# Weights of the edges loaded behind the first three node loads, and prepared one part per node pair

## The reference

```python
q = (x @ Wq + bq).reshape(n, H, C)            # H = 8 heads of C = 32
k = (x @ Wk + bk).reshape(n, H, C)
v = (x @ Wv + bv).reshape(n, H, C)
e = (edge_attr @ We).reshape(-1, H, C)
kj = k[src] + e
alpha = jnp.einsum('ehc,ehc->eh', q[dst], kj) / jnp.sqrt(jnp.float32(C))
amax = jax.ops.segment_max(alpha, dst, num_segments=n)
ea = jnp.exp(alpha - amax[dst])
denom = jax.ops.segment_sum(ea, dst, num_segments=n)
alpha = ea / (denom[dst] + 1e-16)
msg = (v[src] + e) * alpha[:, :, None]
out = jax.ops.segment_sum(msg, dst, num_segments=n)
out = out.reshape(n, H * C) + (x @ Ws + bs)
x = layernorm(x + out)
```

## Time and profile before

| | us |
|---|---|
| median of three runs | 1258.26 |
| lowest and highest | 1256.74, 1258.81 |
| the profiled execution | 1254.81 |
| span of the profiled execution | 1253.0 |

### The profile page before, as it was taken

How to read it: one execution, slowest core, us unless ns; L and a number is a source line. 1 busy time by engine, 2 the same in 40 slices (tenths; PEclk the granted TensorE clock), 3 DMA queues, 4 the chain that set the end, 5 groups by cost and what they waited for, 6 DMA issues and landing times. The chain is left out here.

```text
span 1253.0 us, 26960 instructions
## 1 busy us (share of the span) xinstructions
PE 1207.9 (96%) x7651; PEld 1096.4 (87%) x7651; DVE 1068.5 (85%) x3333; ACT 706.4 (56%) x2263; POOL 825.5 (66%) x747
## 2 busy tenths in 40 slices
PE   7799999999999999999999999999999999999983
PEld 6588888888888888889999999999999889999982
DVE  3789887877878778799999999999999999999983
ACT  2444444555555555556666666666666566666662
POOL 1456656565556656556877778777777777878754
PEclk9899999999999999999999999999999999999996
DMA  6799978778788887843344344444444534444411
GB/s 198 262 293 332 310 277 293 269 265 282 272 281 275 269 285 269 284 166 109 118 119 138 113 136 136 128 150 127 137 137 132 152 118 151 145 129 136 120 57 45
DMA packets 106716, 238.57 MB, mean 190 GB/s; under 512 B 24598, under 2 KB 39114, under 8 KB 106569
## 3 DMA queue, kind: packets, MB, share of 16 engines
q1 hardware_dynamic: 78152, 167.50, 39.9%
q0 software_dynamic: 28416, 69.35, 17.8%
HBM read 156.05 MB, written 88.78 MB: 195 GB/s over the span
## 5 line engine op out<-in xcount | busy, mean ns | idle before, releaser
L532 POOL DMA_INDIRECT rows_in<-xrows_dram,slot x308 | 341.6, 1109 | 85.7 <-issue 82.2
L1135 PE MATMUL bank<-w_y,xT 128*128 128x256 f32 x1568 | 373.2, 384 | 17.2 <-DVEq L752 8.8
L1135 PEld LDWEIGHTS bank<-w_y,xT 128*128 128x128 f32 x1568 | 288.4, 192 | 52.5 <-DVEq L752 8.8
L1155 PE MATMUL bank<-w_kv,sd 128*128 128x512 f32 x1176 | 311.7, 400 | 0.0
L560 POOL DMA_INDIRECT out_dram<-area,where x196 | 220.4, 1124 | 65.1 <-issue 55.3
L626 ACT ACTIVATE square<-y 128x256 f32<-128x256 f32 x392 | 159.8, 409 | 178.4 <-DVE var L833 110.8
L1155 PEld LDWEIGHTS bank<-w_kv,sd 128*128 128x128 f32 x1176 | 210.4, 188 | 37.4
L636 ACT CAST sd<-bank 128x512 fp32r<-128x512 f32 x196 | 115.1, 587 | 188.1 <-PE bank L1147 187.0
L1155 PE MATMUL bank<-w_s,sd 128*128 128x256 f32 x1176 | 190.9, 298 | 0.4 <-DVE area L980 0.4
L523 POOL TENSOR_TENSOR rstd<-var,half 128x4 f32<-128x4 f32 x98 | 111.1, 1133 | 118.8 <-DVE var L833 117.1
L825 DVE TENSOR_TENSOR y<-bank,bias_s 128x512 f32<-128x512 f32 x196 | 134.1, 684 | 64.4 <-PE bank L1135 64.0
(11 more groups left out here) (122 smaller groups left out, 1738.0 us busy)
## 6 DMA issues: line engine op xcount, KB each, us to landing
xT<-xt_dram SPq DMA_DIRECT2D x98, 512.0 KB, 4.6
out_dram<-y SPq DMA_DIRECT2D x98, 512.0 KB, 4.0
eT<-et_dram SPq DMA_DIRECT2D x98, 256.0 KB
dst_all<-dst_row_dram SPq DMA_DIRECT2D x49, 256.0 KB
ahead<-rows_in SPq DMA_DIRECT2D x42, 256.0 KB, 4.8
rows_in<-ahead SPq DMA_DIRECT2D x84, 128.0 KB
rows_in<-xrows_dram,slot POOLq DMA_INDIRECT x392
out_dram<-area,where POOLq DMA_INDIRECT x196
```

The source lines that it names most:

```text
L532: nc.gpsimd.indirect_dma_start(out=rows_in[:, t % RIN, i, :], out_offset=None, in_=xrows, in_offset=bass.IndirectOffsetOnAxis(ap=slot[:, t ...
L1135: ins = nc.tensor.matmul(node_bank(p)[:, i * D:(i + 1) * D], xT[:, u % RX, c, 2 * b + i, :], w_y[:, c, :], start=(c == 0), stop=(c == KC - 1))
L1155: ins = nc.tensor.matmul(to, rows[a][:, c * P:(c + 1) * P], weights[b][:, c, :], start=(first and n == 0), stop=(last and n == len(terms) ...
```

## The change

The loads: `bias_s` gets a semaphore of its own and is issued behind the first node load. All of `load_rest` (four weights, three biases, columns, four flag rows, slots) is issued in one go behind the third node load, ahead of pair 0.

The start on VectorE: it waits for `w_y` alone; takes the mean, subtracts it, then waits for the identity and adds it (the mean takes in the identity as 1.0), signals `consts`, and only then waits for `bias_s` and takes its mean off.

The extras: one per pair from pair 2 on instead of two per pair from pair 7 on, so in pairs 2 to 12.

```diff
-        EXTRAS_FROM = 7
+        EXTRAS_FROM = 2
...
-            k = (p - EXTRAS_FROM) * 2
-            return extras[k:k + 2] if k >= 0 else []
-
-        assert EXTRAS_FROM + len(extras) / 2 <= FRONT
+            k = p - EXTRAS_FROM
+            return extras[k:k + 1] if k >= 0 else []
+
+        assert EXTRAS_FROM + len(extras) <= FRONT
...
             sp.dma_start(w_y[:], ws.rearrange("(c k) n -> k c n", k=P)).then_inc(loaded_y, 16)
-            sp.dma_start(bias_s[:], bs.partition_broadcast(P)).then_inc(loaded_y, 16)
...
-            def load_rest(n):
-
-                if n == 0:
-                    load_weights(0, wk)
-                    load_weights(1, wv)
-                if n == 1:
-                    load_weights(2, wq)
-                    load_weights(3, we)
-                if n == 2:
-                    for i, b in enumerate((bk, bv, bq)):
-                        sp.dma_start(bias_kvq[:, i * D:(i + 1) * D], b.partition_broadcast(P)).then_inc(loaded_w, 16)
-                if n == 3:
-                    sp.dma_start(col_i[:, 0, :], cols[:, 0, :]).then_inc(loaded_i, 16)
-                    load_flags(0)
-                    load_slots(0)
+            def load_rest():
+
+                for i, w in enumerate((wk, wv, wq, we)):
+                    load_weights(i, w)
+                for i, b in enumerate((bk, bv, bq)):
+                    sp.dma_start(bias_kvq[:, i * D:(i + 1) * D], b.partition_broadcast(P)).then_inc(loaded_w, 16)
+                sp.dma_start(col_i[:, 0, :], cols[:, 0, :]).then_inc(loaded_i, 16)
+                load_flags(0)
+                load_slots(0)
...
                 if u + RX < NODE_GROUPS:
                     load_x(u + RX)
-                if u < 4:
-                    load_rest(u)
...
             for u in range(RX):
                 load_x(u)
+                if u == 0:
+                    sp.dma_start(bias_s[:], bs.partition_broadcast(P)).then_inc(loaded_b, 16)
+            load_rest()
             for p in range(FRONT):
                 node_pair(p)
...
-            dve.wait_ge(loaded_y, 16 * 2)
+            dve.wait_ge(loaded_y, 16)
+
+
+            then(nc.vector.tensor_reduce(mean[:, 0:KC], w_y[:], AX.X, ALU.add))
+            then(nc.vector.tensor_scalar(mean[:, 0:KC], mean[:, 0:KC], 1.0, 1.0 / D, ALU.add, ALU.mult))
+            for c in range(KC):
+                then(nc.vector.tensor_scalar(w_y[:, c], w_y[:, c], mean[:, c:c + 1], None, ALU.subtract))
             dve.wait_ge(pool_const, 3)
-
-
             for c in range(KC):
                 diag = w_y[:, c, c * P:(c + 1) * P]
                 then(nc.vector.tensor_tensor(diag, diag, ident[:], ALU.add))
-            then(nc.vector.tensor_reduce(mean[:, 0:KC], w_y[:], AX.X, ALU.add))
+            nc.vector.engine_nop().then_inc(consts, 1)
+            dve.wait_ge(loaded_b, 16)
             then(nc.vector.tensor_reduce(mean[:, KC:], bias_s[:], AX.X, ALU.add))
-            then(nc.vector.tensor_scalar(mean[:], mean[:], 1.0 / D, None, ALU.mult))
-            for c in range(KC):
-                then(nc.vector.tensor_scalar(w_y[:, c], w_y[:, c], mean[:, c:c + 1], None, ALU.subtract))
+            then(nc.vector.tensor_scalar(mean[:, KC:], mean[:, KC:], 1.0 / D, None, ALU.mult))
             then(nc.vector.tensor_scalar(bias_s[:], bias_s[:], mean[:, KC:], None, ALU.subtract))
-            nc.vector.engine_nop().then_inc(consts, 1)
```

More of the change, by code:

```diff
@@ L197, in build @@
         loaded_y = sem("loaded_y")
+        loaded_b = sem("loaded_b")
         loaded_w = sem("loaded_w")
```

## The result

The changed kernel takes 1248.8 us (median of six runs, 1247.4 to 1250.45) against 1258.18 (six runs, 1256.74 to 1258.81): a ratio of 0.9928, with a 95% interval of 0.9915 to 0.9941, or 9.4 us less. That lies in the range of the prediction, 1.7 us under its time of 1250.5.

A forecast was written before the change was run, and what follows sets the result against it. TensorE, busy 96%, bounds the kernel as one chain from its first transpose at 53.65 us. Landing of `bq`, VectorE's work, root and gather give 46.4, 7.2 us sooner: 1250.5 us, range 1247 to 1255.

The forecast's parts named there:

- Part 1: Start: TensorE starts at 6.0 in place of 8.78 us, 2.8 us sooner; worth nothing by itself, only room.
- Part 2: Loads behind the third node load: `bq` lands at 16.8 us and not 28.8, with ends of 15.6 and 19.4.
- Part 3: VectorE from `bq`'s landing to the variance of pair 12: 20.3 us, variance at 37.1 against 44.38, gain 7.2 us.
- Part 4: Other possible delays in the front: TensorE idles 2.3 us before pair 14, 2.7 before the transpose; shift stays 7.2 us.
- The sum: Path to the first transpose: variance of pair 12 at 37.1, plus 1.45 and 7.82, gives 46.4 us.
- T: TensorE's first transpose, at the front's end: forecast at 46.4 us, against 53.65 before.
- F: Rival: `bq` lands at 15.6 us or sooner and the gather is shorter, gain 8.5 to 10 us; chance 0.07.
- A: The forecast: gain 7.2 us, with `bq` landing at 16 to 18.3 us, gains of 5.7 to 8; chance 0.62.
- B: Rival: clock falls in a short idle stretch, first edge slot runs at 1.2 GHz, costing 2.4 us; gain 4.8; chance 0.08.
- D: Rival: gain lost at the edge phase, the gather taking 13 us instead of 7.82; within 2.5 us; chance 0.06.
- E: Rival: VectorE's wait in pair 2 decides; slower if `bq` lands from 24.0 us on, 1 us for each; chance 0.03.
- loss (2): In the front, first matmuls run slowly, 5.30 us for 15 against 5.00 for 25 later, granted clock read as 1.00.

The follow-up runs named there:

- the second set: Changed kernel, unaltered, run again against the kernel before: 1249.22 us against 1256.85, ratio 0.9945.
- those four: Kernel before with loads alone (ratio 1.0049), extras alone (none), start alone (0.9985); changed kernel with old start (0.9951); chip where every kernel took 1,484 to 1,516 us.
- gather first: Changed kernel, but GpSimd starts the gathers of the first two tiles ahead of its root of pair 12: 1249.54 us, ratio 0.9951.
- both: Changed kernel with gathers started ahead of the root of pair 12 and flags 0 moved to pair 24: 1247.18 us, ratio 0.9933.
- the one with 1 MB more: Changed kernel with two unused 512 KB loads ahead of the weights, counted too by VectorE's wait in pair 2: 1252.55 us, ratio 0.9954.
- the kernel without the move of flags 0: Changed kernel, gathers ahead of the root of pair 12, first edge loads behind pair 5 in place of pair 13: 1245.49 us, ratio 0.9912.

## Why the prediction was right, and where it was off

The frame held: the front became 9.7 us shorter, the medians differ by 9.4 (7.6 in the second set), and from the first transpose on the kernel is the same chain of TensorE work. The test that this stretch be unchanged within 1 us failed in the trace, though: it took 1199.4 us before and 1201.6 after, by the fall of the clock at 994.8 us and in the tail. Part by part:

- **Part 1.** TensorE started at 5.88 us (6.0 predicted). But "worth nothing by itself" was wrong: the old start costs the changed kernel 2.2 us at the variance of pair 12. The step that failed is the 1.6 us of waiting for `bq` in pair 2, behind which the start was to be hidden. It did not even follow from the prediction's own numbers: with the old start the addition of pair 2 ends at 18.0 us and `bq` lands at 16.8, so 1.2 us would have shown. In fact the landing (15.1) and the addition of pair 2 (14.9) come together, and with the old start the addition is 2 us late.
- **Part 2.** `bq` landed at 15.14 us, not at 16.8, and below my lower end of 15.6. (That end was itself wrong: its terms, 10.1 + 2.5 + 3.6, give 16.2.) The mis-sized term is that of the three biases: 2.4 us (12.7 to 15.1) and not 3.7. I had taken 1.2 us each from rows in which a store and a node load ran beside them, and 1.9 from the first load of all. The node loads and the weights together were right: 12.7 us against 13.1, though the third node load itself landed at 11.2 and not 10.1, with the weights already beside it.
- **Part 3.** 19.9 us of VectorE, 20.3 predicted. The stretch has 0.86 us of gaps, against 0.97 before.
- **Part 4.** TensorE idled 1.80 us ahead of pair 14 (2.3 predicted) and 1.81 ahead of the transpose (2.7). It waited for no node load in the front, where up to 1 us was allowed for the fourth. The gather took 7.45 us, against the 7.82 carried over.
- **The sum.** T was to be 46.4 us and came at 43.96. The 2.4 us are 1.7 of the landing, 0.4 of VectorE and 0.4 of the gather. The span of the first trace agrees with my 7.2 us only because that execution lost 2.4 us elsewhere. By the median of the first set it is 9.4 us, which is in what I had called F, with a chance of 0.07, and not in A, whose end was 8; the second set's 7.6 us lies in A. The trace of the first set also meets F's conditions (`bq` before 15.6 us, a shorter gather); in that of the second the gather took 8.6 us. The mechanism is the forecast one; which of the two sizes is nearer the truth stays open. That the median came within 1.7 us of 1250.5, although the front was mis-sized by 2.4 us, is in part luck.
- **The rivals.** B is real, in one of two traces of the changed kernel, at 0.9 us and not 2.4. D did not come. E's mechanism is shown by two runs: with the extras alone, VectorE stood 9.8 us in that wait and the kernel's front became longer; and 2.64 us more of landing gave 2.63 us more at the variance of pair 12. Its point of decision was right within 1 us: 53.65 - 28.8 = 24.9 us by the changed kernel's own row of the table, 24.0 predicted.

No part does it alone. In T the loads bring 3.1 us, the start 3.2 and the extras -1.5, together 4.8; all three bring 9.7. The missing 4.9 us lie between the loads and the extras, not with the start: in the kernel with the old start these two bring 6.8 us, where one by one they bring 3.1 and -1.5. Early loads alone leave the extras in pairs 7 to 12; early extras alone leave VectorE waiting for the loads. The start then adds 2.9 us, about what it brings alone. The single figures hold some chance of their own: the pace of the first matmuls, see the end, brought some 0.7 us of the loads' figure, 1.1 of the start's and 1.4 of the extras' (estimates from the traces). The start with only one of the other parts was not run, and what the parts are worth in time, not in T, is not shown, since the ratios of those four tell nothing.

## What to carry to other kernels

Where an engine in order waits for a load and has a fixed queue of work behind it, cost the change as "when does it get past the wait" plus that queue, with everything that was done ahead of the wait added; and check whether the load or the engine's own previous step ends the wait, since an improvement of the other is then hidden only by their difference. Where two parts of a change need each other, as the loads and the extras here, trials of one part at a time mislead: by itself the second looked harmful. Moving loads ahead of others is a trade in one row of transfers: three times here the load that was pushed back became the next wait. The Trainium skill ("DMA: Bandwidth & Descriptors", Rules for kernel authors) advises to issue a load early and wait late; it held for the 1.4 MB put into an empty stretch. For the 1 MB put into one that was 0.6 to 0.8 busy the result is mixed: beside "gather first" it brought 4.5 us of shift, beside "both" nothing, since TensorE then stood 3.2 to 4.5 us for a node load.

## What the hardware did that I had not expected

- The pace of the first matmuls rises at different moments, and it is the clock. The starts of TensorE's first matmuls stand 0.43 us apart, the later ones 0.22. The step falls, in all 14 traces, where the trace's first record of the granted clock begins: at 14.95 us in the kernel before, 11.75 in the changed one, 10.15 in the one with 1 MB more. Ahead of that record there is none, and the views print 1.00 there; so the 1.00 that the prediction reads in its loss (2) is no reading of the clock. Two stretches of the kernel before, of 5 us each, with 14 matmuls in the first and 25 in the second (columns as above):

```profile
9.50:14.50 5.00, 5.00 (x14) 3.92 (x13) 0.69 (x1) 1.12 (x1) 0.00 (x0) 1.00 0.00 2
15.50:20.50 5.00, 5.00 (x25) 4.41 (x24) 2.15 (x4) 2.64 (x13) 1.04 (x1) 1.00 0.74 230
```

  From TensorE's first matmul to that record it is 3.4 us (extras only) to 6.2 us (before), 5.9 in the changed kernel and 4.1 in the one with 1 MB more. Half of the difference between two traces is what their later pairs gain or lose: the addition of pair 2 starts 8.52, 8.37 and 7.49 us after TensorE's first load in the kernel before, the changed one and the one with 1 MB more. This alone moves the front by up to 1.4 us from one trace to the next.
- Nearly every longer pause had a fall of the clock with it. In the first 60 us of the 14 traces, after its first matmul, TensorE paused fourteen times for 2.24 to 6.26 us, and in thirteen of them a stretch at 0.50 began in the pause or at most 1.3 us behind it; the exception is the 3.16 us in the kernel without the move of flags 0. None of the pauses of up to 2.05 us had one, the two of 1.8 us in the first trace of the changed kernel among them. In the two traces of the changed kernel rival B thus went by the gather: a pause of 1.81 us ahead of T in the one, 3.00 us in the other. The 3.4 us at 0.50 from 994.8 us are of another kind, behind no pause at all, and have no cause that these traces show.
- SyncE's issues took longer with many loads outstanding, in order of time:

```profile
3.16 0.43 SPq L368 DMA_DIRECT2D rows_in<-wk_dram  x1
...
4.52 1.27 SPq L368 DMA_DIRECT2D rows_in<-wq_dram  x1
...
7.52 0.98 SPq L375 DMA_DIRECT2D area<-bv_dram  x1
```

Four of them took 0.84 to 1.27 us and a fifth 0.70, in place of 0.43 to 0.47. The last issue of the 13 ended at 12.80 us and not at about 10, which is 0.3 us after VectorE began the addition of pair 1 (12.52), so SyncE did hold the fourth node load up by a little. It had no effect: TensorE never waited for it.
